# Waits between list scatters, and a new order for the residual, the turnings and the output copy in each head

## The reference

```python
x = x + tanh(g_xattn) * xattn(k=ctx, v=ctx, q=layernorm(x))
x = x + tanh(g_ffn) * moe(layernorm(x))

# xattn: i, j are rows of a head (head_dim 8), l the time
kv  = einsum('bhil,bhjl->bijhl', k, v)
y   = irfft(rfft(kv, 2L) * rfft(ssm_kernel, 2L))[..., :L] + kv * D
out = einsum('bijhl,bhil->bjhl', y, q)

# moe: one shared expert, 7 routed ones, top 2 by sigmoid, T/7 tokens at most each
h = x @ w1; x1, x2 = split(h, 2); ffn = x1 * silu(x2) @ w2
```

## Time and profile before

| | |
|---|---|
| Median of three timed runs | 4221.76 us (4221.09 to 4223.56) |
| The profiled execution | 4218.65 us |
| Its span | 4217.0 us |
| First stage | up to about 1850 us |
| TensorE busy | 4023.1 us, 95% of the span |
| VectorE busy | 2717.6 us, 64% |
| ScalarE busy | 1878.8 us, 45% |
| GpSimd busy | 1427.6 us, 34% |
| Mean granted clock of TensorE | 0.979 |

### The profile page before, as it was taken

One profiled execution on the slowest core, in us unless ns is written; L12 is line 12 of the kernel. 1 busy time (PEld: TensorE's weight loads), 2 busy tenths in 40 slices (PEclk: granted clock), 3 DMA queues, 4 the chain that ended last, 5 costly groups with the idle time before them and its releaser, 6 DMA issues.

```text
span 4217.0 us, 68165 instructions
## 1 busy us (share of the span) xinstructions
PE 4023.1 (95%) x24346; PEld 3683.4 (87%) x24346; DVE 2717.6 (64%) x3103; ACT 1878.8 (45%) x2441; POOL 1427.6 (34%) x1275
## 2 busy tenths in 40 slices
PE   8999999999999999989999996199999999999999
PEld 7999999999999999967777875178899998999997
DVE  8999999999999999954545563023334343344342
ACT  7888888888888888731111110011112122122120
POOL 2444444544444444401010004710123333333331
PEclk9999999999999999999999998599999999999999
DMA  7888888888888888855552322142364444445443
GB/s 189 215 213 207 212 215 213 212 208 212 215 212 208 210 213 213 208 150 169 176 176 79 120 74 61 30 99 90 94 158 105 92 106 108 85 107 112 92 92 46
DMA packets 292116, 631.99 MB, mean 150 GB/s; under 512 B 33290, under 2 KB 132074, under 8 KB 291976
## 3 DMA queue, kind: packets, MB, share of 16 engines
q0 software_dynamic: 70096, 250.00, 30.8%
q1 hardware_dynamic: 221880, 380.03, 29.8%
HBM read 344.77 MB, written 136.37 MB: 114 GB/s over the span
## 4 chain that ended last, share of the span: by engine, by line
PE 47%; issue 5%; DVE 2%; ACT 1%; another core or an unknown queue 1%; DMA 0%; SPq 0%; POOL 0%; DVEq 0%; PEldq 0%; POOLq 0%
PE mem_acc L2077 11%; PE mem_acc L2078 10%; PE mem_acc L2079 10%; PE moe_ps L2117 3%; PE moe_ps L2119 3%; PE moe_ps L2118 3%; PE moe_psT L2117 2%; PE moe_psT L2118 2%; PE moe_psT L2119 2%; PE moe_psT L2092 1%; ACT moe_zh L1644 1%; DVE moe_y L1989 0%; DVE moe_zin L1950 0%; DVE moe_zl L1902 0%
## 5 line engine op out<-in xcount | busy, mean ns | idle before, releaser
L2077 PE MATMUL mem_acc<-moe_zh,moe_w1h 128*128 128x512 f32 (+2 forms) x2336 | 850.2, 364 | 16.6 <-issue 8.1
L2078 PE MATMUL mem_acc<-moe_zl,moe_w1h 128*128 128x512 f32 (+2 forms) x2336 | 843.7, 361 | 0.8 <-issue 0.8
L2079 PE MATMUL mem_acc<-moe_zh,moe_w1l 128*128 128x512 f32 (+2 forms) x2336 | 842.7, 361 | 1.5 <-issue 1.5
L871 PE MATMUL mem_acc<-att_kv_hi,att_tz_hi 128*128 128x288 f32 x2560 | 768.5, 300 | 20.4 <-DVE mem_pick L810 17.9
L873 PE MATMUL mem_acc<-att_kv_hi,att_tz_lo 128*128 128x288 f32 x2560 | 756.6, 296 | 0.0
L872 PE MATMUL mem_acc<-att_kv_lo,att_tz_hi 128*128 128x288 f32 x2560 | 755.7, 295 | 0.0
L1975 DVE TENSOR_TENSOR moe_hid<-mem_acc,moe_act_s 128x512 f32<-128x512 f32 (+2 forms) x148 | 91.5, 618 | 768.9 <-PE mem_acc L2079 408.8
L871 PEld LDWEIGHTS mem_acc<-att_kv_hi,att_tz_hi 128*128 128x128 f32 x2560 | 481.9, 188 | 41.0 <-DVE mem_pick L810 17.9
L2077 PEld LDWEIGHTS mem_acc<-moe_zh,moe_w1h 128*128 128x128 f32 x2336 | 440.9, 189 | 71.2 <-issue 32.3
L1658 ACT ACTIVATE moe_act_s<-mem_acc 128x512 f32<-128x512 f32 (+2 forms) x148 | 80.0, 540 | 924.1 <-PE mem_acc L2079 889.2
L872 PEld LDWEIGHTS mem_acc<-att_kv_lo,att_tz_hi 128*128 128x128 f32 x2560 | 482.1, 188 | 0.0
(11 more groups left out here) (242 smaller groups left out, 8592.3 us busy)
## 6 DMA issues: line engine op xcount, KB each, us to landing
att_kv_lo<-att_kv POOLq DMA_DIRECT2D x126, 1152.0 KB, 10.3
att_kT<-in_cT SPq DMA_DIRECT2D x64, 512.0 KB, 8.1
att_xn<-in_x SPq DMA_DIRECT2D x64, 512.0 KB, 5.8
out<-att_x SPq DMA_DIRECT2D x64, 512.0 KB, 5.0
z_d<-att_z SPq DMA_DIRECT2D x256, 128.0 KB
moe_y<-out SPq DMA_DIRECT2D x128, 256.0 KB
moe_raw<-z_d POOLq DMA_DIRECT2D x64, 512.0 KB, 4.5
out<-moe_y SPq DMA_DIRECT2D x128, 256.0 KB
```

What stands on the lines that cost most here:

```text
L871: nc.tensor.matmul(acc, w_hi[:, cols], x_hi, start=start, stop=False, skip_group_check=True)
L2077: nc.tensor.matmul(acc, w1h[j][:, c, b, :], zh[:, c, 0:w], start=(c == 0), stop=False)
L2078: nc.tensor.matmul(acc, w1h[j][:, c, b, :], zl[:, c, 0:w], start=False, stop=False)
L2079: last = nc.tensor.matmul(acc, w1l[j][:, c, b, :], zh[:, c, 0:w], start=False, stop=(c == C - 1))
```

## The change

It makes five edits. Before each list scatter GpSimd waits for the scatter of the previous block on the same list. On TensorE `turn_o(h-1, 0)` goes from behind the second tile to behind the first, and `turn_o(h-1, 1)` from the middle of the sixth tile to behind the second shared product. On VectorE `residual(h-1, 1)` goes behind `multiply(h, 0)`. On ScalarE `conv_out(h, 0)` goes ahead of `normal_x1(h-2)` and `squares(h+1, 0)`. In the last head ScalarE's and VectorE's work on z and w1 for the second stage goes later or is reordered, and SP's first loads of it go ahead of `store_z(h-2)`.

```diff
@@ -383,15 +383,16 @@
             sp.dma_start(out[T:T + P, :], zero[:, :]).then_inc(filters_out, 16)
 
             def step(h, u, ahead, back, back2):
+                if not ahead:
+                    sp.wait_ge(z_out, 64 * (h - 2))
+                    load_ffn_z(0)
+                    load_ffn_z(1)
+                    load_ffn_w1(0)
                 if back2:
                     store_z(h - 2)
                 if not (isinstance(h, int) and h >= H - 2):
                     load_keys(h + 2)
                 if not ahead:
-                    sp.wait_ge(z_out, 64 * (h - 2))
-                    load_ffn_z(0)
-                    load_ffn_z(1)
-                    load_ffn_w1(0)
                     load_ffn_z(2)
                     load_ffn_z(3)
                 if not ahead:
@@ -605,11 +606,11 @@
 
             def step(h, u, ahead, back, back2):
                 more = not (isinstance(h, int) and h >= H - 2)
+                conv_out(h, 0)
                 if back2:
                     normal_x1(h - 2)
                 if ahead:
                     squares(h + 1, 0)
-                conv_out(h, 0)
                 conv_out(h, 1)
                 if ahead:
                     high(h + 1, 1 - u, 0)
@@ -622,24 +623,23 @@
                 normal_x(h, u)
                 if ahead:
                     squares(h + 1, 1)
-                else:
-                    ffn_z_high(0)
-                    ffn_z_high(1)
                 conv_out(h, 4)
                 queries(h, u, 0)
                 if not ahead:
-                    ffn_w1_high(0, 1)
+                    ffn_z_high(0)
+                    ffn_z_high(1)
                 queries(h, u, 1)
                 if ahead:
                     high(h + 1, 1 - u, 1)
                 else:
-                    ffn_z_high(2)
+                    ffn_w1_high(0, 1)
                 conv_out(h, 5)
                 minus_v(h, 1, 0)
                 minus_v(h, 1, 1)
                 if ahead:
                     minus_high(h + 1, 1 - u, 1)
                 else:
+                    ffn_z_high(2)
                     ffn_z_high(3)
                     ffn_w1_high(0, 0)
                 if back:
@@ -828,17 +828,17 @@
                 else:
                     ffn_z_turn(0)
                     ffn_z_turn(1)
+                if not ahead:
                     ffn_z_low(0)
                     ffn_z_low(1)
                     ffn_w1_low(0, 1)
+                    ffn_z_turn(2)
+                    ffn_z_turn(3)
+                multiply(h, u, 0)
                 if back:
                     residual(h - 1, 1 - u, 1)
                 if not ahead:
-                    ffn_z_turn(2)
-                    ffn_z_turn(3)
                     ffn_z_low(2)
-                multiply(h, u, 0)
-                if not ahead:
                     ffn_z_low(3)
                     ffn_w1_low(0, 0)
                 if ahead:
@@ -948,13 +948,11 @@
 
                 def turnings():
                     turn_x(h, 1)
-                    if back:
-                        turn_o(h - 1, 1)
 
                 conv(h, u, 0)
-                conv(h, u, 1)
                 if back:
                     turn_o(h - 1, 0)
+                conv(h, u, 1)
                 conv(h, u, 2)
                 conv(h, u, 3)
                 shared(h, u, 0)
@@ -962,6 +960,8 @@
                 turn_x(h, 0)
                 conv(h, u, 5, turnings)
                 shared(h, u, 1)
+                if back:
+                    turn_o(h - 1, 1)
                 conv(h, u, 6)
                 conv(h, u, 7)
 
@@ -1519,6 +1519,7 @@
             pool.wait_ge(routed, 1)
             for h in range(H):
                 for n in range(2):
+                    wait(pool, scattered[n], 16 * h)
                     nc.gpsimd.indirect_dma_start(list_of[n], bass.IndirectOffsetOnAxis(slot_of[:, h, n:n + 1], 0),
                                                  pay[:, h, n, :], None).then_inc(scattered[n], 16)
             for n in range(2):
```

## The result

The changed kernel takes 4279.11 us (median of three; 4273.29 to 4282.55) against 4221.76: a ratio of 1.0133, interval 1.011 to 1.0156, 1.3% slower and clear of the noise. The forecast was 4221, no change. The profiled execution has a span of 4277.4 us.

The account below looks back on a forecast made before the run. TensorE and VectorE were taken as both near the bound in the first stage; -5 (steady heads) - 4 (last head) + 8 (scatters) = -1 us, forecast 4221 us, range 4080 to 4355.

Parts of the forecast that it names:

- I take the first: Steady heads: GpSimd's mean L441 is held only until L683 ends, loop 27.85 us a head, -5 us in all.
- the three cases of L441: GpSimd's mean after the move: held until L683 ends (-5 us), not held (-26), or held through L725 too (+126).
- The rival with 2.06 us a head: Steady heads: GpSimd's L441 is held through L725 as well, +126 us, 4352 us in all; chance 0.18.
- The transfer waited for has always landed: Scatters: the pacing holds nothing back, as at most two are in flight; its waits cost +8 us.
- rival 2: Scatters: the pacing lifts the crawl of the other engines, worth up to 144 us, 4069 us; chance 0.22.
- is not needed: After the scatters: the list can come later at no cost, since GpSimd waits 276.20 us afterwards for other data.
- TensorE sheds its 0.48 us if conv_out(h,0) is no longer late: Steady heads: TensorE's weight loads lose their 0.48 us a head of waits for ScalarE's L542 and L534.
- VectorE's 0.43 us: Steady heads: the residual's wait for the transposes L941 goes, VectorE's work becomes 27.50 us a head; -26 us if nothing else came.
- The last head: TensorE's 5.20 us wait before L929 goes nearly whole, some comes back at the next product: -4 us, between -8 and +3.
- The first turning: Transposes of o's first half move one tile earlier on TensorE; their input is ready in time, so no cost.
- load_x: SP's load of x is issued later, behind the moved residual, with 2.2 us left: costed at 0, +30 us at the upper end.
- rival 4: Scatters: each one pays 0.51 us more for its wait, +65 us, 4278 us in all; chance 0.10.

Follow-up runs that it names:

- E2: The changed kernel without the waits before the scatters: 4212.28 us against 4074.12 for the kernel before, ratio 1.0332.
- E18: E2's kernel again in a later group: 4213.93 us against 4074.47 for the kernel before, ratio 1.0339.
- E4: Changed kernel plus a VectorE wait for the differences before add_up(h,0): 4087.42 us against 4074.12 for the kernel before, ratio 1.003.
- E6: Kernel before, each scatter waiting for the landing of the one just before it: 4175.4 us against 4223.15, ratio 0.9888.
- E10: Kernel before with a pause every eighth scatter, last-head edits and conv_out(h,0) first on ScalarE: 4062.47 us, ratio 0.9973.
- E9: Kernel before with a pause every eighth scatter and the last-head edits: 4073.39 us against 4074.49, ratio 0.9996.
- E11: Kernel before with a pause every eighth scatter and only turn_o(h-1,0) moved: 4073.84 us against 4074.49, ratio 0.9999.
- E14: E10 with the residual behind the multiplications and E4's wait: 4095.67 us against 4221.75 for the kernel before, ratio 0.97.
- E8: Changed kernel with center moved from GpSimd to VectorE, behind the residual: 4214.83 us against 4223.15 for the kernel before, ratio 0.999.
- E1: Kernel before with only the change's waits before the list scatters added: 4075.45 us against 4074.12, ratio 1.000.
- E5: The changed kernel again, in another group: 4277.42 us against 4223.15 for the kernel before, ratio 1.016.
- E7: Kernel before with a wait for both lists' last scatters before every eighth scatter: 4076.84 us against 4223.15, ratio 0.9653.

## Why the prediction was wrong

**The step that failed** is "I take the first" of the three cases of L441. The rival with 2.06 us a head was the right one; it measured 2.34, 142 us in all and not 126, and E2 and E18 give 138 to 139 by the clock. The loop itself, as that rival sums it, was right to 0.13 us in each term. What was wrong is the rule for letting GpSimd through. I had it that a wait in the next instruction lets it pass. E4 shows that the wait must be one that is still open when VectorE gets there: L725's (for the multiplications) was fulfilled before L683 began, so L725 stood ready while L683 ran, and went first. For the mean, the held instruction takes its turn behind the one in execution and the one standing ready behind it: L712 and L714 before, L683 and L725 after, L683 alone in E4. That isn't a rule for every GpSimd instruction. The trace of the kernel before has one that passed a ready successor, L455, which takes 269 ns at the median of 64:

```profile
1025.62 0.69 DVE L730 TENSOR_TENSOR att_oT<-att_prod 128x512 f32<-128x512 f32 x1
1026.09 0.27 POOL L455 TENSOR_TENSOR att_root<-att_minus_mean,att_root 128x1 f32<-128x1 f32 x1
```

It starts 0.22 us before L730 ends, L691 is ready behind L730 (L522 had ended at 1025.62), and yet L455 is done 0.05 us after L730. The mean started early in the instruction that held it (0.32 and 0.38 us in), L455 in the last third; whether that decides isn't shown. In all these cases two-input instructions of VectorE held a GpSimd instruction that reads SBUF, as the Trainium skill says ("SBUF — State Buffer", Who interferes with whom). The same page's "until the first finishes" (Summary: rules for kernel authors) agrees with L455 and with E4's 1157 ns, and is short by one instruction for the 3274 ns of the changed kernel.

**The scatters** failed in both steps. "The transfer waited for has always landed" came from the one landing that the trace shows, at the end of the crawl, when nothing else moved. With traffic landings are later, 26 waits held, and the change won back 81 us where I had given it a loss of 8. So rival 2 (up to 144) was half right: back-to-back issue does starve the others, but only in some groups, and only where the series stays unbroken for some 20 us or where its mean rate is high; the runs don't part these two. That the list "is not needed" for 276 us was wrong by GpSimd's wait being only one of its readers (E6).

**"TensorE sheds its 0.48 us if conv_out(h,0) is no longer late", costed at nothing:** the edit is worth 11 us alone (E10), by 0.15 us a head at the product behind the transposes; the weight loads' waits, of which the 0.48 us are made, stay. VectorE's 0.43 us was a follower of TensorE's period.

**The last head,** taken at -4: -1 within the noise (E9): what is gained up to 1800 us is lost again by 1850. The 5.20 us did go, and the prediction said that some would come back at the next product; nearly all of it does, at L978, which now waits 6.5 us for ScalarE's copy (in E9; no such wait before, and 6.9 us in the changed kernel):

```profile
PE mem_acc L978 <- ACT att_y L535: 6.5, 1, 6.5
```

**The first turning,** "no cost": right (E11). **load_x,** costed at 0 with 30 us at the end of the range: none in the changed kernel, whose heads are long enough, but 8.3 us in all in E14 and 62.4 in E8. It would have been next.

**The sum:** +142 - 81 = +61 on the span, against -5 - 4 + 8. The 4278 us of rival 4 are met by chance: its mechanism, a dearer issue, isn't there (E1).

What stays open: why the kernel before crawls in some groups of runs and not in others; by how much the pacing alone helps in one that crawls (only the difference is known: 54 us for the whole change in E5, so some 84 if the order costs its 138 there too); and what the crawling engines wait for. From 2595 to 2735 us of the kernel before, the profile names nothing ("issue") that ended ScalarE's two waits, nor one of 21.2 us of TensorE's:

```profile
ACT moe_zh L1644 <- issue: 110.0, 2, 77.3
...
PE moe_psT L2117 <- issue: 22.9, 2, 21.2
```

The version that beats both kernels is E10's: 4061 to 4062 us, 0.3% under the kernel before where that doesn't crawl. Where it does, E10 wasn't run; E7, which lacks its 11 us, is there at 0.9653.

## What to carry to other kernels

When an instruction moves, look at what runs behind it at its new place, and whether the releases that it gives pass through GpSimd: a held GpSimd instruction of 0.26 us cost 3 us here, and one wait that forces a gap on VectorE freed it. An engine that waits for another isn't thereby the bound: move the wait's own cause first and see which period follows. Time a suspicious stall beside a second session before costing its cure, and break long series of indexed transfers into short ones in any case, since it cost nothing here (E11 with the pause: 4073.84 against 4074.49 us where nothing crawls).

## What the runs showed of the hardware

- With one issue every 1.26 us from GpSimd for 20 us or more, TensorE, VectorE, ScalarE and SP can fall to a crawl (17.31 us busy of 100) at which a batch of 68.21 us takes 211.85. Series of 8 (GpSimd busy 57.94 of 100 us) don't do it, of 16 (68.23) do partly, of 32 (73.65) fully; the same dense series does nothing in other sessions (140.00 of 140 us, E2).
- A GpSimd instruction of 264 ns took 1157, 3274 or 3678 ns by what VectorE had in execution and ready; another (L455), started 0.22 us before VectorE's instruction ended, took 269 ns and passed a ready one.
- Waits on semaphores that are already fulfilled were free in front of an indexed transfer: 81 of 127 scatters behind one started 0.3 us after the one before, and E1's time didn't change (4075.45 us against 4074.12).
